# A four-part Flamingo block on one core: the quantised FFN's rounding constant subtracted by ScalarE with GpSimd's bias adds behind it, and the last spiking group on VectorE alone

## What is computed

```
x_q      = round(layernorm(x) * 32767 / amax) ; amax over all of x
hidden   = gelu(x_q @ W_in_q + b_in)
hidden_q = round(hidden * 32767 / max|hidden|)           # one maximum over all 64 batches
x        = x + tanh(g_ffn[0]) * (hidden_q @ W_out_q + b_out)
...
h   = relu(layernorm(x) @ W_fc.T) ** 2
y   = h @ W_proj.T
mem = 0
for 5 steps:
    mem = 0.9 * mem + y - (mem > 1)
    spk += (mem > 1)
out = x + tanh(g_ffn[1]) * spk / 5
```

## Time and profile before

| | |
|---|---|
| runs (3) | 1496.22, 1496.54, 1498.16 us; median 1496.54 |
| the profiled execution | 1496.88 us, span of its instructions 1495.1 us |
| quantised FFN, first and second half | 616 to 679 us, 679 to 744 us |
| spiking FFN | 1361 to 1495 us |
| TensorE's granted clock | 0.999 of full speed over the span |

### The profile page before, as it was taken

The page is one execution under the profiler, slowest core; times in us unless marked ns, Lnnn a source line. Parts: engine busy times, 40 slices in busy tenths (PEclk is TensorE's granted clock), DMA queues, the critical chain, the costliest instruction groups (busy, mean ns, idle before and its releaser), DMA issues. The chain is left out here.

```text
span 1495.1 us, 27545 instructions
## 1 busy us (share of the span) xinstructions
PE 1448.0 (97%) x9408; PEld 1213.3 (81%) x9408; DVE 1081.5 (72%) x2327; ACT 892.3 (60%) x1904; POOL 635.8 (43%) x758
## 2 busy tenths in 40 slices
PE   9999999999999999879999999999999999999997
PEld 8888888888888887638978888888888888778886
DVE  4677877676767678899866666676767666776886
ACT  4666666666666654590056666666666666556662
POOL 1343334343333344572023434343333343455885
PEclk9999999999999999999999999999999999999999
DMA  6655534444444432300065444444444444320011
GB/s 222 189 181 161 165 130 152 140 141 145 143 151 133 153 122 87 88 1 1 4 189 164 134 157 132 157 133 161 133 154 133 154 133 151 107 69 8 28 35 44
DMA packets 202787, 182.72 MB, mean 122 GB/s; under 512 B 12368, under 2 KB 201808, under 8 KB 202640
## 3 DMA queue, kind: packets, MB, share of 16 engines
q1 hardware_dynamic: 202080, 180.91, 38.4%
q10 hardware_dynamic: 576, 0.13, 0.1%
HBM read 95.74 MB, written 85.25 MB: 121 GB/s over the span
## 5 line engine op out<-in xcount | busy, mean ns | idle before, releaser
L1131 POOL TENSOR_TENSOR PN<-E,RC 128x512 f32<-128x512 f32 x378 | 331.3, 905 | 491.8 <-DVE RC L1089 491.8
L1038 DVE TENSOR_REDUCE MX<-pS 128x6 f32<-128x462 f32 (+1 forms) x384 | 222.2, 579 | 265.1 <-PE pS L657 265.1
L772 ACT ACTIVATE G<-pP 128x308 f32<-128x308 f32 (+1 forms) x488 | 209.4, 429 | 226.6 <-PE pP L525 226.3
L695 PE MATMUL pO<-work,PT 128*128 128x128 f32 (+1 forms) x2560 | 328.2, 276 | 4.1 <-ACT PT L856 4.1
L657 PE MATMUL pS<-G,XT 128*128 128x462 f32 (+1 forms) x768 | 320.9, 507 | 0.0
L695 PEld LDWEIGHTS pO<-work,PT 128*128 128x128 f32 (+1 forms) x2560 | 307.6, 191 | 8.4 <-issue 6.1
L847 ACT ACTIVATE E<-E 128x462 f32<-128x462 f32 (+1 forms) x384 | 209.6, 546 | 136.1 <-DVE E L1048 128.0
L523 PE MATMUL pP<-Chi,Ahi 128*128 128x308 f32 x496 | 235.1, 474 | 1.4 <-ACT G L772 1.2
L1048 DVE TENSOR_TENSOR E<-pS,MX 128x462 f32<-128x462 f32 (+1 forms) x384 | 223.4, 582 | 8.9
L856 ACT ACTIVATE PT<-pT 128x512 f32<-128x512 f32 (+1 forms) x384 | 200.6, 523 | 29.9 <-PE pT L680 28.5
L1086 DVE TENSOR_REDUCE SM<-E 128x16 f32<-128x1232 f32 (+1 forms) x144 | 184.8, 1290 | 45.1 <-ACT E L847 44.0
(11 more groups left out here) (230 smaller groups left out, 2020.1 us busy)
## 6 DMA issues: line engine op xcount, KB each, us to landing
values<-ST SPq DMA_DIRECT2D x256, 256.0 KB
work<-values SPq DMA_DIRECT2D x512, 128.0 KB
values<-ST SPq DMA_DIRECT2D x64, 208.0 KB
work<-values SPq DMA_DIRECT2D x128, 104.0 KB
C<-in_ctx SPq DMA_DIRECT2D x32, 154.0 KB
X<-in_x SPq DMA_DIRECT2D x16, 256.0 KB, 5.1
out<-s_O SPq DMA_DIRECT2D x16, 256.0 KB, 2.3
work<-in_L_xattn_Wq SPq DMA_DIRECT2D x2, 512.0 KB, 6.0
```

The costliest lines, as they stand in the source:

```text
L695: last = nc.tensor.matmul(pO[:, 0:CH], PT[0:rows, c, :], V[(t - 1) % VRING][0:rows, tile, CH * hh:CH * hh + CH], start=c == 0, stop=c == C ...
L772: return nc.scalar.activation(G[0:live, g % 2, :, head, :], bank[0:live, 0:KEYCOLS].rearrange("p (b k) -> p b k", k=KEYS), ACT.Copy)
L1038: nc.vector.tensor_reduce(MX[:, h0:h1], pS[u][:, 0:(h1 - h0) * KEYS].rearrange("p (h k) -> p h k", k=KEYS), X_AXIS, ALU.max).then_inc(max_ ...
L1131: nc.gpsimd.tensor_tensor(out, e, scale, ALU.mult).then_inc(prob_ready, 1)
```

## The change

Two parts. In the quantised FFN VectorE only scales and adds the constant, in place in HID (semaphore rounded), and ScalarE subtracts the constant into HQ with a Copy and a bias. VectorE rounds group 2 before the residual of group 0, and so runs one group further ahead. GpSimd waits for the first four rounded blocks before its 16 bias adds. In the spiking FFN group 15 (LAST) has its steps on VectorE alone (turned_stage): a third instruction compares, subtracts the leak and so leaves the membrane with its sign turned, alternating between the buffers Y and MEM; the next step multiplies and compares with the signs turned as well. The counts of groups 14 and 15 have banks of their own and take each mask as it comes; group 14 is weighted by ScalarE and added to X by GpSimd, group 15 is stored by VectorE. The filler in front of these counts is shortened from 18 and 16 to 14 and 8 matmuls.

```diff
 (quantised_ffn, GpSimd)
             pool.wait_ge(gbias_made, 1)
+            pool.wait_ge(rounded, GROUP)
             for g in range(GROUPS):
                 rows = p["X"][:, g * GROUP:(g + 1) * GROUP, :]
 (quantised_ffn, ScalarE, at its end)
+            for b in range(GROUP):
+                n = slice(128 * b, 128 * b + 128)
+                act.wait_ge(rounded, b + 1)
+                nc.scalar.activation(HQ[0][:, :, n], HID[:, 0, :, n], ACT.Copy, bias=-ROUND).then_inc(hq_ready, 1)
+            for g in range(1, GROUPS):
+                act.wait_ge(rounded, GROUP + g)
+                if g >= 2:
+                    act.wait_ge(down_ready, g - 1)
+                nc.scalar.activation(HQ[g % 2][:, :, :], HID[:, g, :, :], ACT.Copy, bias=-ROUND).then_inc(hq_ready, 1)
 (quantised_ffn, VectorE)
             for b in range(GROUP):
                 n = slice(128 * b, 128 * b + 128)
-                nc.vector.tensor_scalar(HQ[0][:, :, n], HID[:, 0, :, n], sh[:, 0:1], ROUND,
-                                        ALU.mult, ALU.add).then_inc(added, 1)
-                dve.wait_ge(added, b + 2)
-                nc.vector.tensor_scalar(HQ[0][:, :, n], HQ[0][:, :, n], ROUND, None, ALU.subtract).then_inc(hq_ready, 1)
+                nc.vector.tensor_scalar(HID[:, 0, :, n], HID[:, 0, :, n], sh[:, 0:1], ROUND,
+                                        ALU.mult, ALU.add).then_inc(rounded, 1)
             def quantise_hidden(g):
-                if g >= 2:
-                    dve.wait_ge(down_ready, g - 1)
-                nc.vector.tensor_scalar(HQ[g % 2][:, :, :], HID[:, g, :, :], sh[:, 0:1], ROUND,
-                                        ALU.mult, ALU.add).then_inc(added, 1)
-                dve.wait_ge(added, GROUP + g + 1)
-                nc.vector.tensor_scalar(HQ[g % 2][:, :, :], HQ[g % 2][:, :, :], ROUND, None,
-                                        ALU.subtract).then_inc(hq_ready, 1)
+                nc.vector.tensor_scalar(HID[:, g, :, :], HID[:, g, :, :], sh[:, 0:1], ROUND,
+                                        ALU.mult, ALU.add).then_inc(rounded, 1)
             quantise_hidden(1)
+            quantise_hidden(2)
             done(nc.vector.tensor_scalar(small[:, :], sh[:, 1:2], gate[:, 0:1], None, ALU.mult))
-            for g in range(2, GROUPS):
-                residual(g - 2)
+            for g in range(3, GROUPS):
+                residual(g - 3)
                 quantise_hidden(g)
+            residual(GROUPS - 3)
             residual(GROUPS - 2)
 (spiking_ffn, TensorE)
+                bank = count_bank(g)
+                if not (isinstance(g, int) and g >= LAST - 1):
+                    wait(pe, o_ready, g)
+                    pe.wait_ge(spiked[half], (i + 1) * STEPS)
                 for k in range(STEPS):
+                    if isinstance(g, int) and g >= LAST - 1:
+                        pe.wait_ge(spiked[half], i * STEPS + k + 1)
-            keep_busy(nc, p, pU[0][:, 0:128], 18)
+            keep_busy(nc, p, pU[3][:, 0:128], 14)
             count(GROUPS - 2, 0, GROUPS // 2 - 1)
-            keep_busy(nc, p, pU[0][:, 0:128], 16)
+            keep_busy(nc, p, pU[3][:, 0:128], 8)
             count(GROUPS - 1, 1, GROUPS // 2 - 1)
 (spiking_ffn, ScalarE, at its end)
+            act.wait_ge(gate_ready, 1)
+            act.wait_ge(counted, LAST)
+            nc.scalar.activation(R[0][:, 0, :], count_bank(LAST - 1)[:, :], ACT.Copy,
+                                 scale=gate[:, 0:1]).then_inc(weighted, 1)
 (spiking_ffn, VectorE; the leak's and mask's waits left out)
+            def turned_stage(k):
+                i, src, out = LAST // 2, (MEM[1] if k % 2 else Y[1]), (Y[1] if k % 2 else MEM[1])
+                sign, compare = (-1.0, ALU.is_lt) if k else (1.0, ALU.is_gt)
+                if k < LATER:
+                    nc.vector.scalar_tensor_tensor(out=LEAK[1][:, :], in0=src[:, :], scalar=sign * BETA, in1=pY[1][:, :],
+                                                   op0=ALU.mult, op1=ALU.add).then_inc(leaked[1], 1)
+                nc.vector.tensor_scalar(SPK[:, 1, k, :], src[:, :], sign * THRESHOLD, None, compare).then_inc(spiked[1], 1)
+                if k < LATER:
+                    nc.vector.scalar_tensor_tensor(out=out[:, :], in0=src[:, :], scalar=sign * THRESHOLD, in1=LEAK[1][:, :],
+                                                   op0=compare, op1=ALU.subtract).then_inc(turned_done, 1)
 (spiking_ffn, GpSimd)
+                if isinstance(g, int) and g == LAST:
+                    reset(LAST - 1, 0, i, 3)
+                    return
-            reset(GROUPS - 1, 1, GROUPS // 2 - 1, 3)
+            pool.wait_ge(weighted, 1)
+            nc.gpsimd.tensor_tensor(O[0][:, :, :].rearrange("p b d -> p (b d)"), R[0][:, 0, :],
+                                    p["X"][:, rows, :].rearrange("p b d -> p (b d)"), ALU.add).then_inc(o_late, 1)
```

More of the change, by code:

```diff
@@ L1238, in quantised_ffn @@
             sem(n) for n in ("step", "spread", "tanh", "scaled", "gbias_made", "biased"))
-        added, hq_ready, down_ready, x_done = (sem(n) for n in ("added", "hq_ready", "down_ready", "x_done"))
+        added, rounded, hq_ready, down_ready, x_done = (sem(n) for n in (
+            "added", "rounded", "hq_ready", "down_ready", "x_done"))
         block = s.enter_context(nc.Block())
@@ L1493, in spiking_ffn @@
         counted, last_rs = sem("counted"), sem("last_rs")
+        gate_ready, turned_done, weighted, o_late, o_last = (sem(n) for n in (
+            "gate_ready", "turned_done", "weighted", "o_late", "o_last"))
+        LAST = GROUPS - 1
         stored = p["stored"]
@@ L1509, in run, with count_bank @@
                     step(2 * i + half, half, i)
+        def count_bank(g):
+            return pU[g - (LAST - 1)] if isinstance(g, int) and g >= LAST - 1 else pC
         def has(g, n):
@@ L1520, in step @@
                 settle(sp, p)
-                sp.wait_ge(o_ready, g + 1)
+                if isinstance(g, int) and g >= LAST - 1:
+                    sp.wait_ge(o_last if g == LAST else o_late, 1)
+                else:
+                    sp.wait_ge(o_ready, g + 1)
                 sp.dma_start(out_dram[bass.ds(g * GROUP, GROUP)].rearrange("b q d -> q b d"),
@@ L1555, in count @@
             def count(g, half, i):
-                wait(pe, o_ready, g)
-                pe.wait_ge(spiked[half], (i + 1) * STEPS)
+                bank = count_bank(g)
+                if not (isinstance(g, int) and g >= LAST - 1):
+                    wait(pe, o_ready, g)
+                    pe.wait_ge(spiked[half], (i + 1) * STEPS)
                 for k in range(STEPS):
-                    last = nc.tensor.matmul(pC[:, :], p["identb"][:, :], SPK[:, half, k, :], start=k == 0,
+                    if isinstance(g, int) and g >= LAST - 1:
+                        pe.wait_ge(spiked[half], i * STEPS + k + 1)
+                    last = nc.tensor.matmul(bank[:, :], p["identb"][:, :], SPK[:, half, k, :], start=k == 0,
                                             stop=k == LATER)
@@ L1654, in _ @@
             dve.wait_ge(tanh, 1)
-            nc.vector.tensor_scalar(gate[:, :], gate[:, :], 1.0 / STEPS, None, ALU.mult)
+            nc.vector.tensor_scalar(gate[:, :], gate[:, :], 1.0 / STEPS, None, ALU.mult).then_inc(gate_ready, 1)
+            def turned_stage(k):
+                i, src, out = LAST // 2, (MEM[1] if k % 2 else Y[1]), (Y[1] if k % 2 else MEM[1])
+                sign, compare = (-1.0, ALU.is_lt) if k else (1.0, ALU.is_gt)
+                if k == 0:
+                    dve.wait_ge(y_out, GROUPS)
+                else:
+                    dve.wait_ge(turned_done, k)
+                if k < LATER:
+                    nc.vector.scalar_tensor_tensor(out=LEAK[1][:, :], in0=src[:, :], scalar=sign * BETA, in1=pY[1][:, :],
+                                                   op0=ALU.mult, op1=ALU.add).then_inc(leaked[1], 1)
+                if k == 0:
+                    dve.wait_ge(counted, LAST - 1)
+                nc.vector.tensor_scalar(SPK[:, 1, k, :], src[:, :], sign * THRESHOLD, None, compare).then_inc(spiked[1], 1)
+                if k < LATER:
+                    dve.wait_ge(leaked[1], i * LATER + k + 1)
+                    nc.vector.scalar_tensor_tensor(out=out[:, :], in0=src[:, :], scalar=sign * THRESHOLD, in1=LEAK[1][:, :],
+                                                   op0=compare, op1=ALU.subtract).then_inc(turned_done, 1)
             def step(g, half, i):
                 before = i if half else i + (-1)
+                if isinstance(g, int) and g == LAST:
+                    turned_stage(0)
+                    stage(LAST - 1, 0, i, 3)
+                    store(LAST - 2, 1, i + (-1))
+                    turned_stage(1)
+                    stage(LAST - 1, 0, i, 4)
+                    for k in range(2, STEPS):
+                        turned_stage(k)
+                    return
                 stage(g, half, i, 0)
@@ L1671, in _ @@
             run(dve, step)
```

(12 more changed lines are left out.)

## The result

The changed kernel takes 1488.59 us (1488.17 to 1489.03, 4 runs) beside 1496.49 us for the kernel before: ratio 0.9945, 95% interval 0.9933 to 0.9956, so 7.9 us less. The profiled execution has a span of 1487.2 us where the one before had 1495.1. VectorE's busy time on the page is 1064.9 us (1081.5 in the earlier trace rows), ScalarE's 923.1 (892.3): a shift of work, which alone says nothing of the end.

What follows compares the result with a forecast made beforehand. TensorE, busy 97%, bounds the kernel, so VectorE's work counts only where TensorE waits; the end is a latency chain. FFN 4.74 plus tail 2.85 is 7.6 us off 1496.54: 1488.9 us, own range 1487.8 to 1490.2 (0.72).

Steps and rivals of the forecast that it cites:

- the down projection: Quantised FFN's second half: TensorE never waits, 3.61 us a group, 16 groups in 57.7 us.
- the tail: Last group of the spiking FFN on VectorE alone: final store 3.26 us earlier, less 0.4, sum 2.85 us.
- (a): Quantised FFN's first half: bias adds no longer stretch two quantise instructions, so the stage ends 1.24 us earlier.
- (b): Head of the down projection: filler sets TensorE's start at 681.70, the last group ends 3.5 us earlier.
- ScalarE's 128x2048: Subtraction in the down projection: 1.85 us from the slope, upper end 2.53, taken as 1.9.
- the fourth rival: Down projection: TensorE waits for ScalarE each group; within 0.2% (0.03), or slower from 4.1 us of ScalarE (0.03).
- rival 2: Down projection falls behind while GpSimd adds: mild form 1489.5 us, strong form 1494.3 us; chance 0.12.
- rival 3: One gain missing: the FFN's 1.24 (1490.1 us) or the tail's (1492.1 us); chance 0.10.
- The add's cost: Tail: GpSimd's new add for group 14 delays step 3's mask by 0.24 (early) to 1.15 (late), taken 0.4 us.
- the turn: Tail: VectorE's compare, subtract and sign change with two SBUF inputs, taken as 0.69 us, bounds 0.6 and 1.2.
- The 0.13 for mask 1: Tail, group 15: mask of step 1 waits 0.13 us behind GpSimd's reset of group 14.
- the price: Tail: by the two-SBUF-input rule, step 2's turn holds the add back: 0.58 us instead of 0.4, 1489.1 us.

Runs made afterwards that it cites:

- e5: Changed kernel with 9 instead of 12 filler matmuls between the maximum's spread and the down projection: 1488.06 us.
- e10: Kernel before without GpSimd's 16 bias adds in the quantised FFN, leaving that layer's output bias out: 1492.74 us.
- e4: Kernel before with only the FFN part of the change, without its wait, so GpSimd's adds start at once and ScalarE subtracts: 1495.43 us.
- e9: Changed kernel with ScalarE's 128x2048 subtraction done twice for each group from the second on: 1492.57 us.
- e3: Kernel before with one more wait: GpSimd's bias adds start behind VectorE's fourth subtraction, ScalarE does nothing new: 1499.12 us.
- e8: Changed kernel with GpSimd's add for group 14 held back until the mask of step 3 of group 15: 1488.98 us.
- e1: Kernel before with only the quantised FFN part changed, the spiking FFN as before: 1491.28 us.
- e6: Changed kernel with the old filler before the two last counts, 18 and 16 matmuls instead of 14 and 8: 1488.92 us.
- e2: Kernel before with only the spiking FFN part changed, the quantised FFN as before: 1494.13 us.
- e7: Changed kernel without any filler before the two last counts: 1488.48 us.
- e11: Changed kernel with 9 filler matmuls in the head and the store of group 13 moved between leak and mask of group 15's step 0: 1487.76 us.
- e12: Changed kernel again, unaltered, run on the same chip as the kernel with 9 filler matmuls and the moved store: 1488.34 us.

## Why the prediction was right, step by step

Predicted 1488.9, measured 1488.6. The mechanism was right in both places, but that the sum came so near is partly luck: the down projection gave 0.5 us and the tail 0.3 more than forecast, and a loss of 0.97 that was not in the sum at all took that back.

- (a), the first half of the FFN: 1.24 forecast, 1.23 by the marks (1.30 less the 0.07 it was ahead). Right.
- (b), the head: start of the products at 680.46 by my sum, 680.37 in the trace (0.07 of it earlier). The filler set it, as said, and e5 confirms that. Right.
- The down projection was mis-sized: I read 54.24 us of the earlier trace rows as TensorE's own pace, 3.61 us a group. It was 3.575. About 0.5 us were waits too short for the profile to name, in every second group. VectorE's residuals in the kernel before, in order of time, start alternately 3.57 and 3.63 apart:

```profile
692.70 0.75 DVE L1439 SCALAR_TENSOR_TENSOR X<-u_pu,small,X 128x512 f32<-128x512 f32 x1 [0.56 <-PE u_pu L1326]
...
696.27 0.75 DVE L1439 SCALAR_TENSOR_TENSOR X<-u_pu,small,X 128x512 f32<-128x512 f32 x1 [0.36 <-PE u_pu L1326]
...
699.90 0.75 DVE L1439 SCALAR_TENSOR_TENSOR X<-u_pu,small,X 128x512 f32<-128x512 f32 x1 [0.42 <-PE u_pu L1326]
```

  After, they are all 3.57 apart. e10 shows that the adds are not the cause, and e4 that it goes with VectorE's subtraction or what was changed along with it; by what way that holds TensorE up is open. FFN in all: 5.28 instead of 4.74.
- ScalarE's 128x2048: 1.9 forecast from the slope, 1.91 in the trace. The threshold of the fourth rival was a little high: e9 loses 4.0 us already at 3.60 us of ScalarE's work a group, since the handing over comes on top, so the break-even with the kernel before comes near 3.9 us of ScalarE's work a group rather than at 4.1 (an estimate: e9 leaves 3.9 us of the gain, which over 15 groups is 0.26 more than its 3.60).
- Rounding beside the adds waits for one add at most (2.34 less 1.28 = 1.06) and TensorE never waits: both forms of rival 2 are refuted, and rival 3 with them, since both gains are there (1.23 and 3.14). The rule of the Trainium skill ("SBUF — State Buffer", Who interferes with whom), an exclusive lock for a whole instruction, agrees with this. e3 shows what the waits cost when two such VectorE instructions a group stand on the path: 4.42 us a group.
- The tail: 2.85 forecast, 3.14 measured. The add's cost was taken as 0.4 and is 0.37, which is luck: 0.4 was a choice between an early and a late case, and the turn that held the add up was not in it. The 0.13 for mask 1 was not paid (its row, at 1477.81, has 0.41, although GpSimd's reset ends at 1477.94 on its own row). The turn takes 0.68 (0.69 forecast). By the Trainium skill's rule on two SBUF inputs (same page, same section) the price was to be 0.58. The trace agrees with the rule, since the add takes 1.36 beside a turn and 1.59 in e8. The price was less for two reasons: the add ended 1.13 us after the turn where the sum had 1.21, and the mask, begun at 1481.34, was done 0.29 after the add's end instead of needing its whole 0.41.
- Not foreseen: 0.97 us lost at the entry of the next layer. 0.33 of it is the landing of the context (TensorE's two waits for C are 0.36 and 0.53 instead of 0.19 and 0.37), 0.64 the step into the attention block, where VectorE's wait is 0.98 instead of 0.34. All engines meet there. In the changed kernel SyncE comes last, because it waits until the attention's bias (308 KB) has been written out; before, SyncE was there 0.9 us ahead of the others. The waits of its queue from 735 to 757 us, before and after:

```profile
SPq L160 <- DMA bias<-MB: 4.2, 1, 4.2
```
```profile
SPq L160 <- DMA bias<-MB: 5.7, 1, 5.7
```

  From issue to landing this transfer takes 4.7 us before and 6.2 after. All 14 profiles fall into two sorts. In the kernel before, e1, e3, e4, e6 and e10 it lands after 4.6 to 4.8 us and VectorE's wait is 0.34; in the changed kernel, e2, e5, e7, e8, e9, e11 and e12 it lands after 5.9 to 6.6 and the wait is 0.8 to 1.3. It does not follow the FFN part, which e1 and e4 have too. It follows the filler in front of the two last counts, 18 and 16 matmuls in the first sort and 14 and 8 or none in the second, and e6 differs from the changed kernel in nothing else. So shortening that filler gave 0.62 us at the end and went, in these profiles, with a loss of 0.64 some 730 us earlier. Why a transfer lands later when the program is a few matmuls shorter far behind it is open; the one other difference that I can name is that the page counts 74 packets on instruction queue q8 in the first sort and 73 in the second.

## What to carry to other kernels

In these traces a VectorE tensor_scalar waits for the GpSimd instruction under way, up to one whole add (1.06 us in the changed FFN), and a GpSimd add waits for a VectorE instruction with two SBUF inputs. Moving one of the two only moves the wait (e3, e8, e11). It pays when the wait lands beside work that another engine covers, and here that took the removal of VectorE's second instruction first. After shortening a head, look at what fills the gap: the filler had become the bound (e5). A block without named waits can still hold short ones: compare its pace with that of the same matmuls elsewhere. And follow marks through the whole program: an edit at its end went with a wait in its middle, and e6's unchanged time was a gain and a loss of the same size.

## What the hardware showed that I had not expected

A Copy of 128x2048 on ScalarE takes 1.91 us, where four of 128x512 in a row take 2.19. Without filler between short counts TensorE's granted clock went to 0.50, and that cost 0.32 us from leak to store: 0.2 for the one matmul on the path, the rest through the later add. In e1 the clock fell even with the old filler in front: its last count takes 1.82 us instead of 1.25, with a granted clock of 0.65 over it and 0.50 from 1485 on, after 1.95 us of idling. The kernel before idles for the same 1.95 and counts in 1.25 at 1.00, so this wait alone does not tell the two apart.
